# Two-stage convolution and rotation kernel: taps spread by matmuls, and a reordered change of stage

## What is computed

```
buf[:, :, POS_IDX] = tap; buf[:, :, NEG_IDX] = -tap      # 16 of 25 places
x = x + conv5x5_depthwise(_gn(x), buf)                   # x1
x = x + einsum('hvc,bchw->bvhw', R, _gn(x))              # R: 64 x 128 x 128
```

## Time and profile before

| | us |
|---|---|
| median of 3 runs | 494.1 |
| the runs | 490.88, 494.1, 494.75 |
| span of the profiled execution | 489.2 |
| the median less that span | 4.9 |
| TensorE, VectorE, ScalarE, GpSimd busy | 413.1, 355.1, 275.0, 239.6 |
| DMA, mean rate | 288 GB/s |

### The profile page before, as it was taken

How to read it: one execution, slowest core, us unless ns; L and a number is a source line. 1 busy time by engine, 2 the same in 40 slices (tenths; PEclk the granted TensorE clock), 3 DMA queues, 4 the chain that set the end, 5 groups by cost and what they waited for, 6 DMA issues and landing times.

```text
span 489.2 us, 8816 instructions
## 1 busy us (share of the span) xinstructions
PE 413.1 (84%) x3168; PEld 215.6 (44%) x3168; DVE 355.1 (73%) x716; ACT 275.0 (56%) x533; POOL 239.6 (49%) x313
## 2 busy tenths in 40 slices
PE   0099968999999999999999999725999977879780
PEld 0055434555555555555555555422444433334330
DVE  3329979999998999979999897623777544455470
ACT  1344536766675665764757676313777754646540
POOL 3394556675675656764767662113444422424220
PEclk9999997999999999999999999956999997999897
DMA  9989899999999999999999999998999999999998
GB/s 136 179 173 214 209 216 227 246 239 236 262 229 252 227 247 250 241 241 228 227 255 231 253 325 342 338 306 160 380 385 417 407 410 419 419 417 415 416 409 315
DMA packets 180442, 140.69 MB, mean 288 GB/s; under 512 B 139760, under 2 KB 141872, under 8 KB 176304
## 3 DMA queue, kind: packets, MB, share of 16 engines
q1 hardware_dynamic: 159264, 106.86, 76.7%
q10 hardware_dynamic: 20656, 33.16, 23.6%
q0 software_dynamic: 480, 0.11, 0.2%
HBM read 72.96 MB, written 67.15 MB: 286 GB/s over the span
## 4 chain that ended last, share of the span: by engine, by line
SPq 30%; PE 27%; DMA 26%; DVE 12%; issue 2%; ACT 0%; DVEq 0%
SPq L198 28%; DMA out_dram<-area 18%; PE ps L583 18%; PE ps L647 8%; DMA area<-in_x_dram 4%; DVE stats L497 4%; DMA x_scratch<-area 3%; DVE area L557 2%; DVE stats L504 2%; SPq L221 2%; DVE area L489 2%; DVE area L486 1%; DMA area<-x_scratch 1%; DVE area L547 0%; SPq L232 0%
## 5 line engine op out<-in xcount | busy, mean ns | idle before, releaser
L583 PE MATMUL ps<-area 64*64 64x496 f32 (+2 forms) x2560 | 282.3, 592 | 6.2 <-POOL area L338 4.6
L583 PEld LDWEIGHTS ps<-area 64*64 64x64 f32 x2560 | 145.5, 134 | 97.1 <-issue 92.2
L338 POOL TENSOR_TENSOR area<-mask,area 128x325 f32<-128x325 f32 x128 | 131.0, 1047 | 61.0 <-DVE area L489 29.0
L647 PE MATMUL ps<-area 128*128 128x512 f32 x256 | 121.7, 626 | 25.7 <-DVE area L557 15.5
L557 DVE TENSOR_TENSOR area<-ps,area 128x512 f32<-128x512 f32 x128 | 82.2, 687 | 59.9 <-DMA out_dram<-area 47.1
L431 ACT ACTIVATE area<-area,affine 128x256 f32<-128x256 f32 x194 | 99.1, 591 | 45.9 <-DVE affine L519 45.9
L456 ACT ACTIVATE area<-area,norm 128x256 f32<-128x256 f32 x157 | 80.7, 591 | 59.2 <-PE ps L647 51.7
L391 POOL TENSOR_SCALAR area<-area,norm 128x256 f32<-128x256 f32 x95 | 52.0, 561 | 95.3 <-PE ps L647 86.3
L497 DVE BATCH_NORM_STATS2 stats<-area 128x6 f32<-128x512 f32 x128 | 80.5, 692 | 23.2 <-DMA area<-in_x_dram 23.2
L415 ACT ACTIVATE area<-ps 64x512 f32<-64x512 f32 x128 | 75.9, 593 | 36.6 <-PE ps L583 34.1
L647 PEld LDWEIGHTS ps<-area 128*128 128x128 f32 x256 | 49.6, 202 | 86.6 <-issue 45.6
(11 more groups left out here) (25 smaller groups left out, 69.9 us busy)
## 6 DMA issues: line engine op xcount, KB each, us to landing
area<-in_x_dram SPq DMA_DIRECT2D x252, 128.0 KB, 4.5
x_scratch<-area ACTq DMA_DIRECT2D x62, 512.0 KB, 6.4
out_dram<-area SPq DMA_DIRECT2D x15, 2048.0 KB, 17.6
area<-x_scratch SPq DMA_DIRECT2D x25, 1024.0 KB, 14.4
area<-x_scratch SPq DMA_DIRECT2D x7, 896.0 KB, 18.5
out_dram<-area SPq DMA_DIRECT2D x2, 1024.0 KB, 10.4
area<-tap_rows SPq DMA_DIRECT2D x8, 142.2 KB
x_scratch<-area SPq DMA_DIRECT2D x2, 512.0 KB, 12.2
```

Of the source, the lines that this page charges most:

```text
L338: last = nc.gpsimd.tensor_tensor(taps[k % TRING][:, c * KW:(c + 1) * KW].rearrange("p d (b r) -> p d b r", r=TAPS), bass.AP(tensor=of_rows ...
L583: last = nc.tensor.matmul(ps[half, bank + c].rearrange("p (j w) -> p j w", j=J)[:, :, outs], taps[k % TRING][rows, (2 * pair + c) * KW + d ...
L647: nc.tensor.matmul(ps[:, m % 6, :], rot_t[u % TURNED][:, h], gn[n % NRING][:, h], start=True, stop=True).then_inc(rotated, 1)
```

## The change

Taps: `line` is transposed by TensorE, VectorE spreads the result over the column offsets (`col_taps`) and makes selection matrices from the identity (`row_pick`); 20 small matmuls in four chunks of channels put the taps of each row phase on all partitions in PSUM, and ScalarE copies them to `row_taps` in nine pieces. No tap goes to DRAM and back. The first two rounds of averages stand elsewhere in TensorE's order, group 0 is normed by three engines (three, three and two images), and `measure(1)` comes behind it.

Change of stage: four granules are loaded early instead of seven, each in three parts (groups 0 to 27, 28 to 30, 31), and five whole ones follow. Group 31 is stored by pairs of channels, three stores from SP and one from ScalarE. Norms are stored to DRAM in batches of eight groups for 0 to 23; those of 24 to 31 are picked from `affine` by eight matmuls and copied to `norm2` by VectorE. The load of `norm2` stands ahead of the early loads. The first two rotations are turned earlier, `measure_sum(31)` stands behind the statistics of round 34, and the last round's mean has a PSUM bank of its own.

```diff
-NBATCH = 7
-LAST = GROUPS - GROUPS % NBATCH
+NBATCH = 8
+PICKED = 8
+LAST = GROUPS - PICKED
...
-EARLY = 7
+EARLY = 4
...
-EARLY_GROUPS = 28
+EARLY_GROUPS = (0, 28, 31, 32)
...
 
         w_landed = sem("w_landed")
...
         line_ready = sem("line_ready")
...
         norm2_stored = sem("norm2_stored")
         norm2_landed = sem("norm2_landed")
...
+        def turn_bank(u):
+            return 2 + u if u < PAIR else 6 + u % 2
...
+        def store_pair(queue, k, pair, n):
+            queue.wait_ge(x1_ready, 2 * k + pair + 1)
+            first = k * GC + 2 * pair
+            queue.dma_start(x1_dram[first:first + 2, n].rearrange("c h j w -> h c (j w)"),
+                            y[k % YRING][n * HALF:(n + 1) * HALF, 2 * pair:2 * pair + 2].rearrange("p c j w -> p c (j w)")
+                            ).then_inc(x1_stored[k % YRING], 16)
...
+        def groups_stored(queue, groups):
+            for k in range(YRING):
+                done = len(range(k, groups, YRING))
+                queue.wait_ge(x1_stored[k], 32 * done + (32 if groups == GROUPS and k == (GROUPS - 1) % YRING else 0))
...
+        def tap_batches():
+            banks = iter((1, 2, 3, 4, 5, 0, 3, 4, 5))
+            for n, (first, last) in enumerate(CHUNKS):
+                per = 512 // (KW * (last - first))
+                for row in range(0, TAPS, per):
+                    yield n, first, last, range(row, min(row + per, TAPS)), next(banks)
...
         @block.sync
...
-                if k == 3:
-                    sp.wait_ge(line_stored[1], 32)
-                    load_taps(sp, 1, 0, taps_landed[2])
-                    load_taps(sp, 1, 1, taps_landed[2])
...
-                if s > NBATCH + 3 and (s - NBATCH - 4) % NBATCH == 0 and s - NBATCH - 4 < LAST - NBATCH:
+                if s >= NBATCH + 4 and (s - NBATCH - 4) % NBATCH == 0 and s - NBATCH - 4 < LAST:
...
-            early, late = slice(0, EARLY_GROUPS * GC), slice(EARLY_GROUPS * GC, C)
-            for k in range(YRING):
-                sp.wait_ge(x1_stored[k], 32 * (EARLY_GROUPS // YRING))
-            for n in range(EARLY):
-                if EARLY_SLOTS[n] < XRING:
-                    sp.wait_ge(x1_ready, 2 * (XRING * ((GROUPS - 1 - EARLY_SLOTS[n]) // XRING) + EARLY_SLOTS[n] + 1))
-                load_granule(n, early).then_inc(in_landed[n], 16)
-                if n == EXTRA + 2:
-                    store_norms(LAST - NBATCH)
-            store(sp, GROUPS - 1)
+            def load_part(part):
+                for n in range(EARLY):
+                    if part == 0 and EARLY_SLOTS[n] < XRING:
+                        sp.wait_ge(x1_ready, 2 * (XRING * ((GROUPS - 1 - EARLY_SLOTS[n]) // XRING) + EARLY_SLOTS[n] + 1))
+                    load_granule(n, slice(EARLY_GROUPS[part] * GC, EARLY_GROUPS[part + 1] * GC)).then_inc(in_landed[n], 16)
+
             sp.wait_ge(norm2_stored, 32 * (LAST // NBATCH))
             sp.dma_start(norm2[0:LAST * GC], norm2_dram[0:LAST * GC]).then_inc(norm2_landed, 16)
-            for k in range(YRING):
-                sp.wait_ge(x1_stored[k], 32 * (GROUPS // YRING))
-
-            for n in range(EARLY):
-                if n == 2:
-                    sp.wait_ge(norm2_landed, 16)
-                    sp.wait_ge(norm2_sent, SENT)
-                load_granule(n, late).then_inc(in_landed[n], 16)
+            groups_stored(sp, EARLY_GROUPS[1])
+            load_part(0)
+            for n in range(2):
+                store_pair(sp, GROUPS - 1, 0, n)
+            groups_stored(sp, EARLY_GROUPS[2])
+            load_part(1)
+            store_pair(sp, GROUPS - 1, 1, 0)
+            groups_stored(sp, GROUPS)
+            load_part(2)
...
-            pool.wait_ge(line_ready, len(POS_IDX + NEG_IDX))
-            store_line(pool, 0)
-            pool.wait_ge(line_stored[0], 32)
-            load_taps(pool, 0, 1, taps_landed[0])
             pool.wait_ge(mask_ready, 2)
...
+                needed = [n for n, batch in enumerate(tap_batches()) if batch[1] < (k + 1) * GC]
+                pool.wait_ge(row_taps_ready, len(needed))
...
-                    at = (k * GC + c) * KW
-                    of_taps = row_taps[:, :, at:at + KW].rearrange("p r d -> p d r")
+                    of_taps = row_taps[:, :, :, k * GC + c].rearrange("p r d -> p d r")
...
-                if group(s + 1) and 0 <= s < FILL:
+                if group(s + 1) and s < FILL:
                     normalise(s + 1)
...
-                if s - 3 in range(LAST, GROUPS):
-                    send_norms(s - 3)
...
             load_half(act, 0, 1)
-            act.wait_ge(line_ready, len(POS_IDX + NEG_IDX))
-            store_line(act, 1)
-            act.wait_ge(line_stored[0], 32)
-            load_taps(act, 0, 0, taps_landed[1])
+            def keep_taps(chunks):
+                for n, (chunk, first, last, rows, bank) in enumerate(tap_batches()):
+                    if chunk not in chunks:
+                        continue
+                    act.wait_ge(taps_picked, n + 1)
+                    nc.scalar.activation(row_taps[:, rows.start:rows.stop, :, first:last],
+                                         ps[:, bank, 0:len(rows) * KW * (last - first)].rearrange(
+                                             "p (r d c) -> p r d c", r=len(rows), d=KW), ACT.Identity
+                                         ).then_inc(row_taps_ready, 1)
+
+            keep_taps((0, 1, 2))
...
-                    for j in range(POOL_J if k else 0, J):
+                    for j in range(POOL_J, J if k else J - FIRST_DVE):
...
+                if s == -1:
+                    keep_taps((3,))
...
+                if s == GROUPS:
+                    act.wait_ge(taps_ready, 2 * GROUPS)
+                    for u in range(PAIR):
+                        keep_rotations(u)
+                    store_pair(act, GROUPS - 1, 1, 1)
...
             nc.vector.memset(half_mean[:], 1.0 / HALF).then_inc(half_mean_ready, 1)
+
+            dve.wait_ge(ident_ready, 2)
+            nc.vector.tensor_reduce(own_col[:], ident[0:TAPS * KW, 0:TAPS * KW].rearrange("p (d r) -> p d r", r=TAPS),
+                                    AXIS.X, ALU.add).then_inc(picks_ready, 1)
+            nc.vector.tensor_reduce(phase[:], ident[0:TAPS * KW, 0:TAPS * KW].rearrange("p (d r) -> p r d", r=TAPS),
+                                    AXIS.X, ALU.add).then_inc(picks_ready, 1)
+            dve.wait_ge(picks_ready, 2)
+            of_phase = phase[:]
+            nc.vector.tensor_copy(phases[:], bass.AP(tensor=of_phase.tensor, offset=of_phase.offset,
+                                                     ap=[of_phase.ap[0], [0, BLOCKS + 2], of_phase.ap[1]])
+                                  ).then_inc(picks_ready, 1)
...
+            dve.wait_ge(picks_ready, 3)
+            for row in range(TAPS):
+                at = TAPS + 2 - row
+                of_rows = phases[:].rearrange("p b r -> p (b r)")[:, at:at + HALF]
+                nc.vector.tensor_copy(row_pick[:, row], bass.AP(tensor=of_rows.tensor, offset=of_rows.offset,
+                                                                ap=[of_rows.ap[0], [0, 2], of_rows.ap[1]])
+                                      ).then_inc(picks_ready, 1)
+
+            dve.wait_ge(line_turned, 1)
+            for n, cs in enumerate((slice(*CHUNKS[0]), slice(CHUNKS[0][1], C))):
+                of_line, of_cols = ps[0:TAPS * KW, 0, cs], own_col[:]
+                nc.vector.tensor_tensor(col_taps[:, :, cs],
+                                        bass.AP(tensor=of_line.tensor, offset=of_line.offset,
+                                                ap=[of_line.ap[0], [0, KW], of_line.ap[1]]),
+                                        bass.AP(tensor=of_cols.tensor, offset=of_cols.offset,
+                                                ap=[*of_cols.ap, [0, cs.stop - cs.start]]),
+                                        ALU.mult).then_inc(col_taps_ready, 1)
+
+            nc.vector.memset(own_group[:], 0.0).then_inc(own_group_ready, 1)
+            dve.wait_ge(own_group_ready, 1)
+            for n in range(2):
...
+                                         ap=[of_half.ap[0], [2 * PICKED * GC + GC, PICKED], [1, GC]]), 1.0
+                                 ).then_inc(own_group_ready, 1)
...
+                if s == -1:
+                    dve.wait_ge(affine_ready, 1)
+                    for j in range(J - FIRST_DVE, J):
+                        last = nc.vector.tensor_scalar(normed[0][:, :, j], xin[0][:, j], affine[:, 0, 0, 0, j:j + 1],
+                                                       affine[:, 0, 0, 1, j:j + 1], ALU.mult, ALU.add)
+                    last.then_inc(normed_dve, 1)
+                    measure(1)
...
                     add(s - 1, 1)
                     dve.wait_ge(x1_ready, 2 * s)
-                    measure_sum(s - 1)
+                    if s < GROUPS:
+                        measure_sum(s - 1)
...
+                if s == GROUPS:
+                    measure_sum(s - 1)
```

(109 more changed lines are left out.)

66 lines of the change are left out of this document (25 added, 41 removed).

## The result

The changed kernel takes 481.5 us (479.8 to 483.0) where the kernel before took 494.4 us beside it: a ratio of 0.9737, interval 0.9692 to 0.9783. That is 12.9 us less, where 17.0 were forecast. The profiled execution after has a span of 479.7 us in a run of 481.52, so 1.8 us lie around it and not the 4.9 taken ahead. The span of 489.2 before fits its kernel's fastest run, 490.88, and not the median, so the two profiles show only 9.5 us of the 12.9. A ratio leaves out runs over 1.5% above the fastest of their kernel; a median keeps them.

| us | before | after | forecast |
|---|---|---|---|
| first convolution | 24.84 | 17.95 | 16 to 19 |
| end of the last convolution | 314.1 | 304.0 | 304.1 |
| from there to the last late loads issued | 16.9 | 15.3 | 9.9 |
| ...

What follows compares the result with a forecast made beforehand. Stage one was taken as bound by the stream of loads, the last stage by bytes. 10 us from the stream plus 7 from the change of stage, 17 in all, took 494.1 to 477.1 us; range 470 to 488.

Steps and rivals of the forecast that it cites:

- 10 us forecast: Stage one: the stream of loads shifts 10 us earlier, 8.5 + 1.5, with ends of 6 and 12.4.
- The picks: Start, on TensorE: 6,400 columns take 7.8 us, a third of it behind the first averages.
- the stream ends last; a start a few us later costs nothing: Stage one: the stream allows an end at 304.1, while TensorE without waits would end at 296 to 299.
- with no waits: Stage one: TensorE's 277.8 us from a start at 16 to 19, some 2 us of half rate, end 296 to 299.
- the +9.9 for all stored: Change of stage: all stored 9.9 us after the last convolution's end in place of +16.9, 7 us earlier.
- the +13.5 given as the worst: Change of stage: latest time for all stored, with 3.1 us of early loads ahead of one piece on SP's queue.
- the forecast's +13.1: Change of stage: the first granule's data comes 13.1 us after the last convolution's end, +9.9 and 3.2 us of landing.
- The last part: Late loads before the first output: four channels, 0.13 MB, take 1.0 us at 125 GB/s; by the skill an estimated 4.8.
- Nine granules at the first output: Bytes up to the first output: five whole granules and the last part take 14.1 of 15.1 us, so nothing is lost.
- Norms: covered: Change of stage: norms ready at +11, before the first granule's data at +13.1, covered by 2 us.
- fewer early loads cost what they give: Rival at the change of stage: 2.75 MB not loaded early costs 6.9 us in the last stage, 491.0 us; chance 0.08.
- GpSimd is no bound: Answers a rival in stage one: spreads doubled to 2.1 us make GpSimd the bound, 506 us; chance 0.04.

Runs made afterwards that it cites:

- the kernel with both delays: Changed kernel with the first convolution held until group 3 of x landed and ten loads put back on SP's queue: 491.9 us, ratio 0.9918.
- the late stream: Changed kernel with ten loads of the old tap loads' size put back on SP's queue behind group 3's loads: 490.9 us, ratio 0.9923.

## Why the prediction was right, and where it was not

The time, the sign and the stage that gives most were right; 4.1 us of the 17.0 did not come.

- **Stage one, right in size.** 10 us forecast, 10.1 measured (304.0 against 304.1), with the first convolution at 17.95 (16 to 19) and a `spread_taps` at 1.045 us (1.047 taken). To meet it within 0.1 us is luck: eight profiles with this stage one ended it between 304.0 and 307.9 us, 306.2 in the mean, with stalls for a load in some; the two with the earlier one at 314.1 and 317.4. The picks, 12.2 us in all where 7.8 were reckoned, were mis-sized and did hold the start, by some 2.1 us in front of the first average and 1.2 in front of the first convolution.
- **Stage one, wrong in its reason.** The step "the stream ends last; a start a few us later costs nothing" failed: 6.9 us of later start cost 7.5 at the end. TensorE did wait 5.8 us as forecast (5 to 8), but for `spread_taps` (1.4), issue (2.6) and one `affine` behind VectorE's own statistics (1.8), not for loads and not several times; from 72.9 on it never waited, and SP waited 7.6 us for slots. Of the 10.1 us, 6.9 are the earlier start and 3.2 a shorter run behind it (286.1 against 289.3), near the 3.4 us, an estimate, that 6.8 us at half the clock took before. The stream is a limit too, as its own delay showed. I had summed TensorE's 277.8 us from the first convolution "with no waits", which left it 5 to 8 us of room; the waits use that room, whatever causes them.
- **The change of stage, mis-sized.** 7 us forecast, with ends of 3.4 and 8.5; the profiles show 1.3 up to the first output and none to the end. The step that failed is the +9.9 for all stored: it was +15.3, past the +13.5 given as the worst. That worst priced the bytes of the part ahead of SP's store (3.1 us) and not SP's wait for the stores of groups 28 to 30 in front of that part. With the store first and one late part, the forecast's +13.1 is met (+13.2).
- **The last part.** I took 1.0 us for its 0.13 MB by 125 GB/s. The four loads landed between 322.3 and 326.2, 1.3 us for each, so 5.2 in all. The Trainium skill (SBUF — State Buffer, "Door 1: The DMA port swizzle"), cited for an estimate of 4.8 us, is borne out: 4 channels took as long as 16.
- **Nine granules at the first output.** I took nothing and kept 2.2 us for the range; 1.9 were lost (145.0 against 143.1). With four early granules 143.5 to 145.4 us follow the first output in the kernels tried on the change, with seven 143.0 to 143.4.
- **Norms: covered, right.** They were there at +10.05 (+11 forecast).
- **Rivals.** That fewer early loads cost what they give is refuted by seven against four, by 5.7 us with one late part and 10.7 with two. So the rule of the Trainium skill (DMA: Bandwidth & Descriptors, "Rules for kernel authors") to issue early did not hold at this place, where the early loads stand ahead of the stores on which the rest depends; behind the first output early loads gave 1.9 us back, in the kernel before 3.9. Its large pieces agree with the runs: one late part in place of two brought the first use 2.8 us forward, though the totals aren't told apart. GpSimd is no bound.

What stays open: how much of the 12.9 us the change of stage gives. Between the medians of the kernel with both delays and the kernel before lie 3.3 us, between their profiled spans and stages none. The profiles put the gain in stage one: 9.6 us between the means of its ends (eight and two profiles), while behind it the four profiles with the new order at the change of stage took 174.9 to 175.9 us and the one before 175.1. One profile before can't settle the rest. How far the stream alone would have let stage one end earlier wasn't measured either.

## What to carry to other kernels

Where an engine and the stream of loads that feeds it keep the same pace within one per cent, ask for both what a delay of the start costs at the end: waits that look like slack for one may be the other's, and a gain needs both moved. Loads that are issued early to save time later are paid for where a store that the rest depends on is queued behind them; count them up to that store, and put the store ahead of every wait on its queue. Splitting a load by partitions so that the last piece is small saves nothing where, as here, a quarter of the bytes takes the same time.

## What the runs showed of the hardware

- A load of 4 partitions and 32 KB took 3.05 us from issue to use, one of 16 partitions and 128 KB 3.38; eight small ones held the engines at a share of 0.94 with 111 GB/s. An 8 KB packet took 1.20 us amid loads of 16 channels and 0.31 in whole granules.
- Around a wait of 4.7 to 5.4 us in the middle of stage one TensorE's granted clock was 0.50 for 6.8 us (before, and with the late stream); after the change, where its longest wait there was 1.79 us, it was 1.00 from 21.4 us to the stage's end.
- Engines that look idle are not free to fill: with stores in flight, two loads of 112 channels more brought the share from 0.66 to 1.03 in the 5 us from +5.1 on and pushed the next landings back by 4 us.
